# Turning P for two heads with one DMA transpose, a shorter drain, and full-height operands for two small matmuls

## The chip, the cores and the metric

The kernel runs on one core of one Trainium2 chip. The metric is the device time of one execution in microseconds (us). A core has TensorE (PE, matmuls; PEld is its weight load), VectorE (DVE), ScalarE (ACT), GpSimd (POOL), and SyncE (SP), which here issues every DMA. SBUF is the core's on-chip memory; matmul results land in PSUM, in eight banks.

## The reference

Three layers run one after the other on x (4 batches of 128 rows, width 512), each added to x:

```python
x = x + cross_attention(layernorm(x), ctx)   # ctx: 4 x 2048 x 512, 16 heads of 64, q and k RMS-normed,
                                             # keys past a batch's length masked
x = x + self_attention(layernorm(x))         # qkv with a bias, causal over 128 rows, output projection with a bias
x = x + ffn(layernorm(x))                    # 512 -> 1536 -> 512, gated, 4-bit weights and 16-bit activations by rounding
```

In the cross attention, K and V of each batch are `ctx @ Wk` and `ctx @ Wv`, the scores are `q k^T / 8`, P is their softmax over 2048 keys, the head's output is `P @ V`, and the heads' outputs are multiplied by Wo. Nearly all of the arithmetic is there: 4 x 2048 rows of context go through two 512 x 1024 projections.

## The kernel before

Every fp32 operand of a matmul is split into a high and a low fp16 part, and each product is three matmuls: high by high, high by low, low by high. Each stage (`cross_attention`, `self_attention`, `feed_forward`) is a block: one hand-written instruction list for each engine, tied by semaphores, and a barrier of all engines at its end.

**The loop over slots.** Cross attention goes over 4 batches, 8 groups of two heads and 4 chunks of 512 keys. That is 128 projections (`PROJS`), each spread over two slots, so there are 256 slots with projections; a part n is one head of one chunk, and there are 256 parts (`PARTS`). Eight parts (two heads, four chunks) are a unit. In slot s each engine does the steps whose lag fits: PE projects half a chunk of K and V (24 matmuls of 256 columns, L144 to L146), multiplies P by V for part s - 18 (`values`, `PV_LAG`, L824 to L826), and in odd slots makes the scores of a chunk for both heads (L868). In between, DVE masks the scores and takes their maximum (L703), ACT takes the exponential (L597) and copies it to fp16, the high half (L620), and POOL subtracts for the low half (L513). SP turns P with a DMA transpose of the 1024 columns (high and low) of one part (L397), into one of three buffers, and PE reads it as the stationary operand of `values`. Once in a unit, `values` opens with a matmul of zeros into its PSUM bank (L820), whose operands have one row each. K takes a way of its own: DVE sums its squares (L718), POOL takes the root (L523), DVE scales K (L724), and another DMA transpose (L404) turns it. ACT's high half of a part waits until the DMA transpose of the part three before has landed.

**What shares the queue.** SP's list also holds, in program order, the loads of the context, of the queries of a unit (`q_now`, L434) and of weights, and the storing of prepared weights in DRAM. Where an instruction waits, all behind it wait.

**The drain.** Projections end with slot 255, P by V of the last part comes in slot 273. The last 16 parts are turned by PE instead (L888), copied out of PSUM by DVE (L785). Two 512-column matmuls in each of five slots (L876) have no other use than to keep PE working. From slot 262 on (`OUT_FIRST`) PE also does the output projection of the first three batches, a quarter of a batch (six matmuls of 512 columns, L905 to L907) in each slot. The tiles of Wo for it come back from DRAM after slot 255, because they go where the context's low half lies. The block ends when the last unit's output has been divided (L684, L687), split (L643, L548) and sent through a DMA transpose (L459).

**Self attention** starts with the query and key projections (L1094 to L1096), has the last batch's output projection after seven of them (L1119), and adds the value bias with two matmuls of one-row operands ahead of each of the eight value projections (L1106, L1107). The attention of each batch goes through DMA transposes of P (L990) and of the output (L995), and its output projection (L1119) reads the latter.

## Time and profile before

| | |
|---|---|
| median of 3 runs | 1226.51 us (1225.75 to 1233.3) |
| the profiled execution's own time | 1228.04 us |
| its span, first to last instruction | 1226.1 us |
| PE busy | 1161.4 us, 95% of the span |
| DVE, ACT, POOL busy | 814.8, 735.0, 874.3 us |
| cross attention's loop, drain | to about 926 us, to about 971 us |
| self attention, feed-forward | to about 1093 us, to the end |

A matmul is pipelined: the next one starts before the last one's result is complete. So the cost of a matmul in a dense stretch is read from the distance between two starts, and not from its duration. Idle time of an engine matters only where another engine then waits for it.

### The profile page before, as it was taken

To read this page: it belongs to the slowest core of one execution; us is meant where nothing else is said; L and a number is where in the kernel's file an instruction comes from. 1 tells how busy PE (TensorE), PEld (TensorE's weight loads), DVE (VectorE), ACT (ScalarE), POOL (GpSimd) and SP (SyncE) were. 2 spreads that over 40 slices of the span, in tenths; PEclk is the share of its full clock that TensorE was granted. 3 is DMA by queue.
4 is the path that set the end of the run, shared out by engine and by line. 5 is a ranking of instruction groups with operands and counts; after the bars stand their busy time and mean duration, and the time that the engine had idled before them with its cause. 6 is when DMAs were issued, how large, how long until landed. Compare 5 with 4: busy or idle time off the path is not lost. (4 is left out here: it accounts for less than half of the span.)

```text
span 1226.1 us, 31362 instructions
## 1 busy us (share of the span) xinstructions
PE 1161.4 (95%) x11841; PEld 876.1 (71%) x11845; DVE 814.8 (66%) x1780; ACT 735.0 (60%) x1329; POOL 874.3 (71%) x750
## 2 busy tenths in 40 slices
PE   6899999999999999999999999999998899979958
PEld 4677777877888888788888878788885667534423
DVE  5778777697766678676666877666655444542772
ACT  5366655775767667666666776667666336512760
POOL 2689999888888898788888888898887423510510
PEclk9999999999999999999999999999999999989979
DMA  6579999999999999999999998999999533972000
GB/s 208 147 136 187 210 179 192 187 227 207 185 208 193 199 189 217 236 178 202 199 189 203 215 206 178 198 182 216 191 161 238 152 88 70 236 163 39 1 1 35
DMA packets 562345, 209.98 MB, mean 171 GB/s; under 512 B 506770, under 2 KB 529298, under 8 KB 562196
## 3 DMA queue, kind: packets, MB, share of 16 engines
q1 hardware_dynamic: 562196, 207.98, 84.4%
q8 instruction: 95, 1.56, 0.5%
q14 instruction: 54, 0.44, 0.1%
HBM read 66.27 MB, written 23.07 MB: 73 GB/s over the span
## 5 line engine op out<-in xcount | busy, mean ns | idle before, releaser
L144 PE MATMUL pair<-arena 128*128 128x256 f16 x2048 | 559.8, 273 | 15.6 <-DVE arena L655 7.8
L146 PE MATMUL pair<-arena 128*128 128x256 f16 x2048 | 558.9, 273 | 0.0
L145 PE MATMUL pair<-arena 128*128 128x256 f16 x2048 | 558.8, 273 | 0.0
L513 POOL TENSOR_TENSOR p_parts<-probs,p_parts 128x512 f16<-128x512 f32 x256 | 307.7, 1208 | 19.8 <-ACT p_parts L620 19.4
L523 POOL TENSOR_TENSOR k_rinv<-k_ms,half_neg 128x8 f32<-128x8 f32 x128 | 226.3, 1768 | 103.4 <-DVE k_ms L718 102.6
L144 PEld LDWEIGHTS pair<-arena 128*128 128x128 f16 x2048 | 200.2, 98 | 90.7 <-issue 47.7
L703 DVE CUSTOM_DVE_ANT_0 probs<-bank,mask 128x512 f32<-128x512 f32 x256 | 175.1, 684 | 114.8 <-PE bank L868 110.1
L620 ACT ACTIVATE p_parts<-probs 128x512 f16<-128x512 f32 x256 | 160.9, 629 | 100.7 <-DMA pt<-p_parts 89.2
L146 PEld LDWEIGHTS pair<-arena 128*128 128x128 f16 x2048 | 200.4, 98 | 23.7
L145 PEld LDWEIGHTS pair<-arena 128*128 128x128 f16 x2048 | 200.4, 98 | 20.8
L597 ACT ACTIVATE probs<-probs,neg_max 128x512 f32<-128x512 f32 x256 | 182.9, 714 | 8.7 <-DVE neg_max L712 8.7
L624 ACT ACTIVATE k_lh<-k_n 128x512 f16<-128x512 f32 x128 | 80.3, 627 | 152.0 <-DVE k_n L724 151.5
L518 POOL TENSOR_TENSOR k_lh<-k_n,k_lh 128x512 f16<-128x512 f32 x128 | 162.3, 1268 | 10.7 <-ACT k_lh L624 10.6
L724 DVE TENSOR_TENSOR k_n<-pair,k_rinv 128x512 f32<-128x512 f32 x128 | 88.3, 690 | 72.1 <-issue 45.1
L824 PE MATMUL bank<-v_hi,pt 128*128 128x65 f16 x1024 | 119.7, 193 | 2.8 <-DMA pt<-p_parts 2.8
L825 PE MATMUL bank<-v_lo,pt 128*128 128x65 f16 x1024 | 119.6, 194 | 0.0
L826 PE MATMUL bank<-v_hi,pt 128*128 128x65 f16 x1024 | 118.5, 193 | 0.0
L868 PE MATMUL bank<-kt,q_now 64*128 64x512 f16 x744 | 101.9, 379 | 7.2 <-DVE chunk_max L703 4.5
L824 PEld LDWEIGHTS bank<-v_hi,pt 128*128 128x128 f16 x1024 | 94.8, 97 | 10.5 <-DMA pt<-p_parts 4.7
L825 PEld LDWEIGHTS bank<-v_lo,pt 128*128 128x128 f16 x1024 | 94.8, 97 | 2.9
L826 PEld LDWEIGHTS bank<-v_hi,pt 128*128 128x128 f16 x1024 | 95.2, 98 | 0.0
L588 ACT ACTIVATE k_sq<-pair 128x512 f32<-128x512 f32 x128 | 75.1, 586 | 31.9 <-PE pair L146 31.1
(276 smaller groups left out, 1878.0 us busy)
## 6 DMA issues: line engine op xcount, KB each, us to landing
raws<-in_ctx_t_dram SPq DMA_DIRECT2D x64, 256.0 KB, 3.3
side_kept<-side_parts SPq DMA_DIRECT2D x40, 256.0 KB, 3.7
arena<-side_kept SPq DMA_DIRECT2D x40, 256.0 KB, 4.5
w_kept<-ffn_turned SPq DMA_DIRECT2D x36, 256.0 KB, 3.4
side_raw<-in_w_qkv_dram SPq DMA_DIRECT2D x24, 256.0 KB, 3.3
arena<-w_kept SPq DMA_DIRECT2D x24, 256.0 KB, 4.0
pt<-p_parts SPq DMA_TRANSPOSE x240, 3.7
ffn_raw<-in_w_gate_dram SPq DMA_DIRECT2D x12, 256.0 KB, 3.6
```

Of the source, the lines that this page charges most:

```text
L144: nc.tensor.matmul(to, x_hi[k], w_hi[k], start=(k == 0), stop=False)
L145: nc.tensor.matmul(to, x_hi[k], w_lo[k], start=False, stop=False)
L146: mm = nc.tensor.matmul(to, x_lo[k], w_hi[k], start=False, stop=(k == n - 1))
L513: nc.gpsimd.tensor_tensor(p_parts[n % PTS][:, 1, :], probs[n % PROBS][:, :], p_parts[n % PTS][:, 0, :], ALU.subtract).then_inc(p_lo_done, 1)
L518: nc.gpsimd.tensor_tensor(k_lh[(d - 1) % 2][:, 1, :], k_n[:, :, :, :].rearrange("p t h e -> p (t h e)"), k_lh[(d - 1) % 2][:, 0, :], ALU.s ...
L523: nc.gpsimd.tensor_tensor(k_rinv[d % 2][:, :], k_ms[d % 2][:, :], half_neg[:, 0:2 * TILES], ALU.pow).then_inc(k_rinv_done, 1)
L597: nc.scalar.activation(probs[n % PROBS][:, :], probs[n % PROBS][:, :], ACT.Exp, scale=S_SCALE, bias=neg_max[head_of(n) % 4][:, 0:1]).then_ ...
L620: nc.scalar.activation(p_parts[n % PTS][:, 0, :], probs[n % PROBS][:, :], ACT.Copy).then_inc(p_hi_done, 1)
L703: nc.vector.tensor_tensor_reduce(probs[m % PROBS][:, :], scores[h][:, :], mask[:, k, :], 1.0, LOWEST, ALU.add, ALU.max, chunk_max[h][:, k: ...
L824: nc.tensor.matmul(to, hi, v_hi[at % VS][:, t, h, :], start=False, stop=False)
L825: nc.tensor.matmul(to, hi, v_lo[at % VS][:, t, h, :], start=False, stop=False)
L826: mm = nc.tensor.matmul(to, lo, v_hi[at % VS][:, t, h, :], start=False, stop=(n % 8 == 7 and t == TILES - 1))
```

## The change

- P of both heads of a chunk is turned by one DMA transpose of 2048 columns, issued once both low halves are there. `values` comes one slot later (`PV_LAG` 19), P has four buffers in two pairs instead of three, and V ten instead of eleven.
- The tiles of Wo are laid out so that each one replaces two tiles of the context, and are loaded one in a slot from slot 249 on. The output projections start at slots 258, 262 and 266, and slot 257 alone keeps its two idle matmuls.
- The last unit's division, split and transpose move to the start of self attention's block.
- The operands of the zero matmul have 128 rows, not one. The high and the low part of the value bias stand in two rows of one 128-row operand (the rest is multiplied by zero), so one matmul adds both.

```diff
-SCORE_LAG, EXP_LAG, PV_LAG = 7, 15, 18
-CTX_RAWS, KTS, VS, PROBS, PTS, QS = 4, 3, 11, 10, 3, 3
+SCORE_LAG, EXP_LAG, PV_LAG = 7, 15, 19
+CTX_RAWS, KTS, VS, PROBS, PTS, QS = 4, 3, 10, 10, 4, 3
...
-OUT_FIRST, NORM_AT = (262, 266, 270), (266, 270)
+OUT_FIRST, NORM_AT, WO_FIRST = (258, 262, 266), (262, 266), 249
...
-        wo_at = arena[:, 24576:32768].rearrange("p (a k n) -> p a k n", a=2, k=GROUPS)
+        wo_at = arena[:, 24576:32768].rearrange("p (k a n) -> p a k n", a=2, k=GROUPS)
...
-        p_parts = [sb(f"p_parts{i}", [P, 2, CHUNK], F16, c) for i in range(PTS)]
-        pt = [sb(f"pt{i}", [P, 2 * TILES, P], F16, c) for i in range(PTS)]
+        pair_parts = [sb(f"pair_parts{i}", [P, 2, 2, CHUNK], F16, c) for i in range(PTS // 2)]
+        pair_turned = [sb(f"pair_turned{i}", [P, 2, 2 * TILES, P], F16, c) for i in range(PTS // 2)]
+        p_parts = [pair_parts[i // 2][:, i % 2, :, :] for i in range(PTS)]
+        pt = [pair_turned[i // 2][:, i % 2, :, :] for i in range(PTS)]
...
-        zeros = sb("zeros", [1, 2 * VW], F16, c)
+        zeros = sb("zeros", [P, 2 * VW], F16, c)
...
-        LAST = PARTS + PV_LAG + 4
+        LAST = PARTS + PV_LAG
 
         def whole_unit(lag, slot):
 
             n = part(PV_LAG + lag, slot)
-            return n // 8 if n is not None and n % 8 == 7 else None
+            return n // 8 if n is not None and n % 8 == 7 and n < PARTS - 1 else None
...
-                if (n := part(EXP_LAG + 1, slot)) is not None and n < PE_TURNS:
+                if (n := part(EXP_LAG + 1, slot)) is not None and n < PE_TURNS and n % 2 == 1:
+                    at = n // 2 % 2
                     sp.wait_ge(p_lo_done, n + 1)
                     wait(sp, pv_done, n - PTS + 1)
-                    sp.dma_start_transpose(pt[n % PTS][:, :, :],
-                                           p_parts[n % PTS][:, :, :].rearrange("p a k -> p (a k)")).then_inc(pt_in[n % PTS], 16)
+                    sp.dma_start_transpose(pair_turned[at][:, :, :, :].rearrange("p h a q -> p (h a) q"),
+                                           pair_parts[at][:, :, :, :].rearrange("p h a k -> p (h a k)")).then_inc(pt_in[at], 16)
...
+                if 0 <= (j := slot - WO_FIRST) < GROUPS:
+                    if j == 0:
+                        for i in range(2):
+                            sp.wait_ge(side_kept_done[i], 16 * SIDES // 2)
+                    sp.wait_ge(proj_done, PARTS - GROUPS + 1 + j)
+                    sp.dma_start(side_home(j), side_kept[j].rearrange("p (a n) -> p a n", a=2)).then_inc(side_in[j // 4], 16)
                 if slot == PARTS:
                     sp.wait_ge(proj_done, PARTS)
-                    for i in range(2):
-                        sp.wait_ge(side_kept_done[i], 16 * SIDES // 2)
-                for j in range(2 * (slot - PARTS), 2 * (slot - PARTS) + 2):
-                    if 0 <= j < DRAINED:
+                for j in range(GROUPS + 2 * (slot - PARTS), GROUPS + 2 * (slot - PARTS) + 2):
+                    if GROUPS <= j < DRAINED:
...
-                        wait(act, pt_in[n % PTS], 16 * (n // PTS))
+                        wait(act, pt_in[n // 2 % 2], 16 * (n // PTS))
...
-                        pe.wait_ge(pt_in[n % PTS], 16 * (n // PTS + 1))
+                        pe.wait_ge(pt_in[n // 2 % 2], 16 * (n // PTS + 1))
...
-                        nc.tensor.matmul(bank[7][:, 0:2 * VW], zeros[0:1, 0:P], zeros[0:1, :], start=True, stop=False)
+                        nc.tensor.matmul(bank[7][:, 0:2 * VW], zeros[:, 0:P], zeros[:, :], start=True, stop=False)
...
-                        pe.wait_ge(k_n_done, PROJS)
-                        pe.wait_ge(v_lo_done, PROJS)
+                        pe.wait_ge(k_n_done, PROJS - (b < 2))
+                        pe.wait_ge(v_lo_done, PROJS - (b < 2))
...
-        ones = sb("ones", [P, P], F16, c)
-        bv_row = [t[0:1, :, :].rearrange("p h e -> p (h e)") for t in o_n]
-        bv_hi, bv_lo = (sb(n, [P, E], F16, c) for n in ("bv_hi", "bv_lo"))
+        two_rows = sb("two_rows", [P, P], F16, c)
+        bv_row = [t[:, :, :].rearrange("p h e -> p (h e)") for t in o_n]
+        bv_parts = sb("bv_parts", [P, E], F16, c)
...
-                sp.dma_start(bv_row[i], g["b_qkv"][2 * E + D * i:2 * E + D * (i + 1)].partition_broadcast(1)).then_inc(bv_in, 16)
+                sp.dma_start(bv_row[i], g["b_qkv"][2 * E + D * i:2 * E + D * (i + 1)].partition_broadcast(P)).then_inc(bv_in, 16)
...
+            sp.wait_ge(last_lo_done, 1)
+            sp.dma_start_transpose(ot[:, B - 1, :, GROUPS - 1, :], last_parts[:, :, :].rearrange("p a n -> p (a n)")).then_inc(ot_in[1], 16)
...
+            nc.gpsimd.memset(two_rows[:, :], 0.0).then_inc(zeroed, 1)
             nc.gpsimd.memset(v_hi[:, :, :, HD:VW], 1.0).then_inc(ready, 1)
             nc.gpsimd.memset(v_lo[:, :, :, HD:VW], 0.0).then_inc(ready, 1)
-            pool.wait_ge(zeroed, 2)
+            pool.wait_ge(zeroed, 3)
+            for i in range(2):
+                pool.wait_ge(zeroed, 3 + i)
+                nc.gpsimd.affine_select(out=two_rows[:, :], in_=two_rows[:, :], compare_op=ALU.not_equal, fill=1.0, base=-32 * i,
+                                        pattern=[[0, P]], channel_multiplier=1).then_inc(zeroed, 1)
...
+            pool.wait_ge(last_hi_done, 1)
+            nc.gpsimd.tensor_tensor(last_parts[:, 1, :], last_o[:, :, :].rearrange("p h e -> p (h e)"), last_parts[:, 0, :],
+                                    ALU.subtract).then_inc(last_lo_done, 1)
...
+                if at[key] == 1:
+                    pe.wait_ge(last_o_done, 1)
...
-                nc.tensor.matmul(to[:, :], ones[0:1, :], bv_hi[0:1, n * D:(n + 1) * D], start=True, stop=False)
-                nc.tensor.matmul(to[:, :], ones[0:1, :], bv_lo[0:1, n * D:(n + 1) * D], start=False, stop=False)
+                nc.tensor.matmul(to[:, :], two_rows[:, :], bv_parts[:, n * D:(n + 1) * D], start=True, stop=False)
...
-            act.wait_ge(ready, 5)
+            act.wait_ge(last_o_done, 1)
+            act.wait_ge(ot_in[1], 16 * (B * GROUPS // 2 - 1))
+            nc.scalar.activation(last_parts[:, 0, :], last_o[:, :, :].rearrange("p h e -> p (h e)"), ACT.Copy).then_inc(last_hi_done, 1)
...
+            nc.vector.reciprocal(last_rec[:, :], last_new[:, :, HD]).then_inc(last_rec_done, 1)
+            dve.wait_ge(last_rec_done, 1)
+            nc.vector.tensor_tensor(last_o[:, :, :], last_new[:, :, 0:HD], last_rec[:, :].unsqueeze(2).to_broadcast([P, 2, HD]),
+                                    ALU.mult).then_inc(last_o_done, 1)
```

SP's list around the end of a unit, before (pt and kt are the turned P and K, `q_now` the next unit's queries, `ot` a unit's turned output):

```order
L404 DMA_TRANSPOSE kt<-k_lh 128x8x128
L397 DMA_TRANSPOSE pt<-p_parts 128x8x128
L434 DMA q_now<-q_kept 128x2x128
L452 DMA side_raw<-in_wo_dram 128x512
L455 DMA side_kept<-side_parts 128x1024
L459 DMA_TRANSPOSE ot<-o_parts 128x2x128
L397 DMA_TRANSPOSE pt<-p_parts 128x8x128
L404 DMA_TRANSPOSE kt<-k_lh 128x8x128
```

and now:

```order
L408 DMA_TRANSPOSE kt<-k_lh 128x8x128
L446 DMA_TRANSPOSE ffn_turned<-row_parts 128x8x128
L401 DMA_TRANSPOSE pair_turned<-pair_parts 128x16x128
L438 DMA q_now<-q_kept 128x2x128
L456 DMA side_raw<-in_wo_dram 128x512
L459 DMA side_kept<-side_parts 128x1024
L408 DMA_TRANSPOSE kt<-k_lh 128x8x128
```

Two transposes of P to one of K have become one; the queries' load stands right behind it, as it stood behind that of the odd part.

DVE's list in the drain, around the last two maxima (L703, now L711) and the first batch's sum (L793, now L801), before:

```order
L703 ISA probs,chunk_max<-bank,mask 128x512
L703 ISA chunk_max 128x1
L708 TENSOR_REDUCE head_max<-chunk_max 128x1
L712 TENSOR_SCALAR neg_max<-head_max 128x1
L785 COPY pt<-bank 128x1024
L785 COPY pt<-pair 128x1024
```

and now:

```order
L793 COPY pair_turned<-pair 128x1024
L801 SCALAR_TENSOR_TENSOR resid<-pair,resid 128x512
L804 BN_STATS ln_stats<-resid 128x6
L806 BN_AGGR ln_mean_var<-ln_stats 128x2
L711 ISA probs,chunk_max<-bank,mask 128x512
L711 ISA chunk_max 128x1
L716 TENSOR_REDUCE head_max<-chunk_max 128x1
```

The first batch's sum now stands ahead of the last maximum, and no longer four copies behind it.

SP's list where cross attention ends (the branches are the end of one block and the start of the next), before:

```order
L472 DMA arena<-side_kept 128x2x512 x2
L464 DMA_TRANSPOSE raws<-row_parts 128x8x128
L459 DMA_TRANSPOSE ot<-o_parts 128x2x128
L153 UNCONDITIONAL_BRANCH
L976 UNCONDITIONAL_BRANCH
L979 DMA att_o_n<-in_b_qkv_dram 1x512 x2
L980 DMA b_out_rows<-in_b_out_dram 128x512
```

and now:

```order
L463 DMA_TRANSPOSE ot<-o_parts 128x2x128
L468 DMA_TRANSPOSE raws<-row_parts 128x8x128
L155 UNCONDITIONAL_BRANCH
L987 UNCONDITIONAL_BRANCH
L990 DMA att_o_n<-in_b_qkv_dram 128x512 x2
L991 DMA b_out_rows<-in_b_out_dram 128x512
L1014 DMA_TRANSPOSE ot<-o_parts 128x2x128
```

The last unit's transpose has moved from ahead of the block's end to behind the next block's first three loads.

## Rows read from the trace of the kernel before

**Rows 1.** Windows: us, busy time (count) of each engine, granted clock, DMA share, GB/s.
```profile
100.00:920.00 820.00, 808.86 (x9067) 659.97 (x9065) 589.97 (x1316) 553.41 (x982) 716.51 (x573) 1.00 1.02 198
1046.00:1076.00 30.00, 27.75 (x272) 14.73 (x270) 18.12 (x36) 14.95 (x37) 14.28 (x16) 1.00 1.07 237
```
**Rows 2.** Waits of PE from 100 to 920 us: total us, times, longest.
```profile
PE bank L824 <- DMA pt<-p_parts: 2.8, 6, 0.7
PE bank L868 <- DMA q_now<-q_kept: 1.6, 2, 1.1
```
**Rows 3.** Timeline of PE around a zero matmul: start, duration, instruction.
```profile
602.99 0.27 PE L145 MATMUL pair<-arena 128*128 128x256 f16 x1
603.10 0.27 PE L146 MATMUL pair<-arena 128*128 128x256 f16 x1
603.30 0.23 PE L820 MATMUL bank<-zeros 1*128 1x130 f16 x1
603.46 0.20 PE L824 MATMUL bank<-v_hi,pt 128*128 128x65 f16 x1
```
**Rows 4.** SP's transposes of P, 1024 columns (L397): issue in ns, who waited, landing.
```profile
L397 SPq DMA_TRANSPOSE pt<-p_parts x240: 1231/1272/3078, 69.5 to 926.1; - x120
  ACT p_parts L620: 89.2, 68
DMA to landing us min/median/max: 3.0/3.7/6.1
```
**Rows 5.** The same view for the transposes of a unit's output, 256 columns (L459).
```profile
DMA to landing us min/median/max: 2.3/3.7/5.9
```
**Rows 6.** Timeline: the low half of odd part 151 (POOL), and its P by V (PE).
```profile
618.10 1.15 POOL L513 TENSOR_TENSOR p_parts<-probs,p_parts 128x512 f16<-128x512 f32 x1
...
626.82 0.27 PE L146 MATMUL pair<-arena 128*128 128x256 f16 x1
626.93 0.19 PE L824 MATMUL bank<-v_hi,pt 128*128 128x65 f16 x1
```
**Rows 7.** Timeline of PE in the drain, the last three scores, with the wait ahead.
```profile
929.43 0.82 PE L868 MATMUL bank<-kt,q_now 64*128 64x512 f16 x6 [1.63 <-DVE chunk_max L703]
...
934.74 0.82 PE L868 MATMUL bank<-kt,q_now 64*128 64x512 f16 x6 [1.14 <-DVE chunk_max L703]
...
939.27 0.80 PE L868 MATMUL bank<-kt,q_now 64*128 64x512 f16 x5 [1.12 <-DVE chunk_max L703]
```
**Rows 8.** Timeline where cross attention ends and self attention starts.
```profile
966.29 0.38 PE L907 MATMUL pair<-arena,ot 128*128 128x512 f16 x1
...
967.79 1.24 SPq L459 DMA_TRANSPOSE ot<-o_parts  x1
...
971.00 0.37 PE L1094 MATMUL bank<-raws,arena 128*128 128x256 f16 x1 [4.33 <-PEq L90]
```
**Rows 9.** Timeline where self attention ends and the feed-forward layer starts.
```profile
1091.40 0.69 DVE L1333 TENSOR_REDUCE x_tops<-raws 128x1 f32<-128x512 f32 x1
...
1093.04 0.55 SPq L1468 DMA_DIRECT2D wd<-w_kept  x1
```
**Rows 10.** Windows of three stretches, columns as in rows 1.
```profile
925.80:929.20 3.40, 2.00 (x34) 1.25 (x32) 1.82 (x4) 2.92 (x5) 1.95 (x3) 1.00 1.02 186
...
970.20:973.60 3.40, 2.60 (x13) 1.84 (x14) 1.57 (x3) 0.00 (x0) 2.71 (x9) 0.50 0.20 63
...
1076.00:1079.40 3.40, 3.40 (x10) 1.20 (x9) 0.03 (x1) 0.02 (x1) 1.15 (x1) 0.50 0.89 43
```
**Rows 11.** Timeline of PE ahead of the third output projection of self attention.
```profile
1075.51 0.38 PE L1119 MATMUL bank<-arena,ot 128*128 128x512 f16 x1 [2.15 <-issue]
```
**Rows 12.** Timeline of PE around the first value bias.
```profile
998.29 0.27 PE L1096 MATMUL bank<-raws,arena 128*128 128x256 f16 x1
998.49 0.38 PE L1106 MATMUL bank<-bv_hi,ones 1*128 1x512 f16 x1
...
999.02 0.39 PE L1110 MATMUL bank<-arena,raws 128*128 128x512 f16 x1
```

More of the change, by code:

```diff
@@ L129, in program @@
             o_parts = [sb(f"o_parts{i}", [P, 2, P], F16, attn) for i in range(2)]
+            o_rec = [sb(f"o_rec{i}", [P, 2], F32, attn) for i in range(2)]
+            o_n = [sb(f"o_n{i}", [P, 2, HD], F32, attn) for i in range(2)]
             row_parts = [sb(f"row_parts{i}", [P, 2, D], F16, attn) for i in range(2)]
@@ L157, in cross_attention @@
             g[n] for n in ("resid", "ot", "xt", "wo_at", "w_qkv_at", "side_kept", "side_in", "ot_in", "xt_in", "o_parts", "bqk"))
-        o_rec = [sb(f"o_rec{i}", [P, 2], F32, c) for i in range(2)]
-        o_n = [sb(f"o_n{i}", [P, 2, HD], F32, c) for i in range(2)]
+        o_rec, o_n = g["o_rec"], g["o_n"]
         side_raw = [sb(f"side_raw{i}", [P, D], F32, c) for i in range(2)]
@@ L239, in cross_attention @@
         kt_in = sems(c, "kt_in0 kt_in1")
-        pt_in = sems(c, " ".join(f"pt_in{i}" for i in range(PTS)))
+        pt_in = sems(c, "pt_in0 pt_in1")
         v_hi_done, v_lo_done = sems(c, "v_hi_done v_lo_done")
@@ L679, in _ @@
                 d = slot // 2 - 1
-                if (n := part(PV_LAG + 1, slot)) is not None and n % 8 == 7:
+                if (n := part(PV_LAG + 1, slot)) is not None and n % 8 == 7 and n < PARTS - 1:
                     u = n // 8
@@ L919, in self_attention @@
         HALF, TURNED = 2 * P, 11
+        last_o, last_rec, last_parts = g["o_n"][1], g["o_rec"][1], g["o_parts"][1]
+        last_new = bank[7][:, 0:2 * VW].rearrange("p (h v) -> p h v", h=2)
         NORMS = [("out", 2), ("out", 3)] + [("again", b) for b in range(B)]
@@ L956, in self_attention @@
         w_out_in = sems(c, "w_out_in0 w_out_in1")
+        last_rec_done, last_o_done, last_hi_done, last_lo_done = sems(c, "last_rec_done last_o_done last_hi_done last_lo_done")
         pt_in = sems(c, " ".join(f"att_pt_in{i}" for i in range(3)))
@@ L1024, in _ @@
             nc.gpsimd.memset(beyond[:, :, :], 0.0).then_inc(zeroed, 1)
-            nc.gpsimd.memset(ones[:, :], 1.0).then_inc(ready, 1)
+            nc.gpsimd.memset(two_rows[:, :], 0.0).then_inc(zeroed, 1)
             nc.gpsimd.memset(v_hi[:, :, :, HD:VW], 1.0).then_inc(ready, 1)
             nc.gpsimd.memset(v_lo[:, :, :, HD:VW], 0.0).then_inc(ready, 1)
-            pool.wait_ge(zeroed, 2)
+            pool.wait_ge(zeroed, 3)
[3 more added lines that the diff above has]
+                                        pattern=[[0, P]], channel_multiplier=1).then_inc(zeroed, 1)
             nc.gpsimd.affine_select(out=less[:, :], in_=less[:, :], compare_op=ALU.not_equal, fill=-2.0 ** 20, base=0,
@@ L1102, in values @@
                 if b == 0 and n == 0:
-                    pe.wait_ge(ready, 5)
+                    pe.wait_ge(zeroed, 5)
+                    pe.wait_ge(ready, 4)
                     pe.wait_ge(bv_lo_done, 2)
                 to, s, cols = placed(("v", b, n)), slice(b * P, (b + 1) * P), slice(2 * E + n * D, 2 * E + (n + 1) * D)
-                nc.tensor.matmul(to[:, :], ones[0:1, :], bv_hi[0:1, n * D:(n + 1) * D], start=True, stop=False)
-                nc.tensor.matmul(to[:, :], ones[0:1, :], bv_lo[0:1, n * D:(n + 1) * D], start=False, stop=False)
+                nc.tensor.matmul(to[:, :], two_rows[:, :], bv_parts[:, n * D:(n + 1) * D], start=True, stop=False)
                 for k in range(KD):
@@ L1262, in _ @@
                     for h in range(2):
-                        nc.scalar.activation(bv_hi[0:1, D * h:D * (h + 1)], bv_row[h], ACT.Copy, scale=W2_UP).then_inc(bv_hi_done, 1)
+                        nc.scalar.activation(bv_parts[:, D * h:D * (h + 1)], bv_row[h], ACT.Copy, scale=W2_UP).then_inc(bv_hi_done, 1)
                 if i == 10:
                     x_high(1)
+            act.wait_ge(ready, 4)
             high_v(0, 0)
@@ L1369, in _ @@
                         dve.wait_ge(bv_hi_done, h + 1)
-                        nc.vector.scalar_tensor_tensor(bv_lo[0:1, D * h:D * (h + 1)], bv_row[h], W2_UP, bv_hi[0:1, D * h:D * (h + 1)], ALU.mult,
-                                                       ALU.subtract).then_inc(bv_lo_done, 1)
+                        nc.vector.scalar_tensor_tensor(bv_parts[32:64, D * h:D * (h + 1)], bv_row[h][32:64], W2_UP,
+                                                       bv_parts[32:64, D * h:D * (h + 1)], ALU.mult, ALU.subtract).then_inc(bv_lo_done, 1)
                 if i == 8:
```

## The prediction

> **What bounds the kernel now.** I read the windows first. From 100 to 920 us PE is busy for 808.9 of 820 us and the clock stays at its full level [rows 1], so there a change is worth what it takes from PE's own list; POOL, next, is busy for 716.5. The waits of PE say how little is left for a faster supply: in those 820 us it waits 2.8 us for turned P and 1.6 us for the queries [rows 2]. Then I looked for what a busy share hides, by the distance between two starts in the timeline [rows 3]. The places where PE really stands lie after the loop: three waits for the maxima in the drain, 4.33 us at the end of cross attention, and a wait of 2.15 us in self attention, each with its rows below.
>
> **The zero matmul.** A projection matmul starts 0.11 us after the one before; the one-row zero matmul starts 0.20 us after its predecessor, and the next starts 0.16 us behind it [rows 3]. With 128 rows it should take its share of columns, 130/256 of 0.11, which is 0.06, and the start ahead of it should go back to 0.11. That saves 0.09 + 0.10 = 0.19 us. There is one in each of 32 units, 30 of them in the dense loop: **-5.8 us** (between nothing and -6.2). I take the full saving because the same 0.09 us stands ahead of the one-row bias matmul too, and matmuls of equal height follow one another without it [rows 3]; the bias is taken up below.
>
> The Trainium skill ("TensorE: Matmul & The Clock Gate", Part 2, step-by-step) speaks against this: time goes by the columns, and "row count K doesn't matter here". By that rule this term would be nothing, and the sum about 6 us longer. The trace differs where the height changes from one matmul to the next, 0.20 against 0.11 us, and I go by the trace.
>
> **One transpose for two parts.** SP issues 120 instead of 240; each issue takes 1.23 us or more [rows 4]. That frees 1.2 us of SP in every two slots (one slot is about 3.4 us), but SP does no work of the loop's bound. The bytes are the same. The landing of 1024 columns takes 3.0 us at least, of 256 columns 2.3 [rows 4, 5]; another 1024 columns add between 0.7 x 1024/768 = 0.9 us and, if all behind the issue doubles, 3.0 - 1.2 = 1.8. So 2048 columns land after 3.9 to 4.8 us at best; with the 0.7 us that the median lies above the least, 4.6 to 5.5. I take 5. The even part's P by V is one slot later than before, and so stands where the odd part's stood: in the example its start is 626.93 - 619.25 = 7.7 us behind the end of the odd part's low half [rows 6]. 5 us and a wait of up to 2 for SP's turn fit into this; the odd part has a slot more. ACT's wait for the part three before, 89.2 us over 68 waits [rows 4], goes for odd parts and gets up to 1.5 us longer for even ones; behind it POOL works off a backlog, which covers that. The queries' load stands right behind the pair and gets up to 1.5 us more of data ahead of it; PE waits for it twice, by at most 1.1 us [rows 2], and the saved 1.2 us of issue is on the other side. Fewer waits for P (2.8 us) against somewhat longer ones for the queries: **-1 us**, between -4 and +6 (about six units at 1 us each). Ten V buffers cost nothing: ACT's copy of chunk d needs the projection of slot 2d + 1 in any case, and PE has read chunk d - 10 in slot 2d, ahead of it in its list.
>
> **The drain.** Only differences count. Eight of ten idle matmuls go, each 0.22 us, twice the 0.11 of 256 columns: -1.8. The output projection of the first batch, 24 x 0.22 = 5.3 us, now stands where PE waited 1.14 and 1.12 us for the maxima [rows 7]: -2.3; the wait of 1.63 us comes ahead of slot 258 and stays. The second zero matmul of the drain gives -0.2. Against that, the eighth tile of Wo can be asked for only when the last projection is done, and lands about when PE is ready for it: +0.5. The last five slots have no projection beside them, and the last copies of P from PSUM are in the open: +0.5. The part moved out of the loop into the drain is neutral. The first batch's sum, now ahead of the last maximum on DVE, delays the exponentials of one head by some 2 us; they are two slots early. So PE ends 3.3 us sooner relative to the loop.
>
> Then the block's end. Before, PE stood for 4.33 us, because the issue of the last unit's transpose ran until 967.79 + 1.24 = 969.03, and PE restarted at 971.00 [rows 8]: 2.0 us from the last instruction to the next block. At the next block's end it is 0.95 us (1092.09 to 1093.04) [rows 9]. Now PE's own P by V is the last work, so its gap is 1.0 to 2.0 us; with 1.4, **-2.9**. The drain together: **-6.2 us**, between -2.5 and -8.5. What is late next is PE itself.
>
> **The clock.** After the 4.33 us gap the granted clock is at its lower level until 973.6 [rows 10], and twelve matmuls start 0.21 instead of 0.11 us apart. After the gap of 1.63 us it stayed full, after that of 2.15 us it fell [rows 7, 10, 11]. A gap of 1.4 us is on the good side: **-1.2**, and nothing if it falls all the same.
>
> **Self attention.** The value bias takes 999.02 - 998.49 = 0.53 us and 0.09 ahead of it [rows 12]; one matmul of 128 rows takes 0.22. That is 0.40 for each of eight. The first three come before attention proper is under way: **-1.2**. The other five lie ahead of the wait of 2.15 us for a turned output [rows 11], in a stretch where the DMA engines are full, 1.07 [rows 1], and only lengthen it; all eight would be -3.2. The moved work of the last unit is DVE 0.5, ACT 0.3, POOL 0.4 us and a transpose of at least 2.3 us [rows 5]; behind POOL's preparations it lands about 7.5 us into the block, and its reader comes after seven projections of 12 x 0.11, at 9.2 us. It costs nothing unless these are late by 1.7 us.
>
> **The sum**: -5.8 - 1.0 - 6.2 - 1.2 - 1.2 = -15.4 on the profiled execution's 1228.0 us (span 1226.1), so 1212.6. That execution lay 1.5 us above the median of 1226.5, so I predict **1211 us**.
>
> **The rivals.** (a) The longer transpose takes back what the zero matmul gives: queries and P late by 0.5 to 1 us in a good part of the units, +6 to +8 on my sum, 1217 to 1219. For it speaks the DMA share of 1.02 [rows 1], against it the room of 7.7 us. Chance 0.17. (b) Height makes no difference, the rule above read as a mechanism of this kernel: the 0.20 and 0.16 us belong to the change of target bank and not to the one row. Then the zero matmuls give nothing (+6.0 with the drain's) and the bias matmuls 0.22 each instead of 0.40 (+0.5): 1217.5. Against it, P by V goes to another bank too and follows at 626.93 - 626.82 = 0.11 where no zeros stand between [rows 6]. Chance 0.07. (c) Slower than before: one transpose of 2048 columns has a price of its own, so that it lands more than the 7.7 us after the odd low half. From there every pair makes PE wait, and 120 waits cost 12 us for each 0.1 us. The point is a landing of about 7 us from issue, twice the median of 3.7 or nearly so; at a mean wait of 0.25 us it is 1211 + 30 = 1241. Against it, 256 columns and 1024 differ by 0.7 us [rows 4, 5]. Chance 0.06. (d) The freed SP queue lets the stalls in the loop go altogether, PE has 11 us of non-busy time there [rows 1], and more of the bias is passed on: -4 to -7, 1204 to 1207. Chance 0.15. (e) My sum within 3 us, 0.55.
>
> The range holds (e), (d) and most of (a) and (b): **1204 to 1220**. What can be told from no change here is about 1%, 12.3 us: faster means below 1214.2. That is (e) for the most part, and (d): **0.65**. The same: (a), (b), the upper end of (e), **0.29**. Slower: (c), **0.06**.
>
> **What would show it.** In the profile after: zero matmuls 0.11 us behind their predecessor and 0.06 ahead of the next; landings of the 2048-column transposes near 5 us and PE's waits for them below 5 us in total; ACT's waits for P fewer than 68; PE standing 1 to 2 us at the end of cross attention, at the full clock afterwards; self attention's start 6 us sooner relative to the loop's end; a wait ahead of the third output projection of self attention longer than 2.15 us. Wrong would be the sum if PE waits for P in every second slot, if the first output projection waits for Wo by more than 2 us, or if self attention ends no sooner relative to its start than before.

## The result, and the profile after

| | before | after |
|---|---|---|
| median | 1229.45 us (20 runs, 1225.75 to 1235.31) | 1225.86 us (20 runs, 1222.39 to 1230.9) |
| ratio | | 0.997, 95% interval 0.9957 to 0.9983 |
| span of the profiled execution | 1226.1 us | 1222.2 us |

(The 20 runs of before take in the three shown ahead, whose median was 1226.51.) The change is worth 3.6 us, not 15. The forecast of 1211 us, with 1204 to 1220 around it, was wrong. Four stages of the two profiled executions show where; a stage ends with the start of the next PE instruction named. (Loop: to the last projection matmul. Drain: to the first matmul of self attention. Self attention: to the last one before the feed-forward layer.)

| us | loop | drain | self attention | feed-forward |
|---|---|---|---|---|
| before | 925.9 | 45.1 | 120.9 | 134.2 |
| after | 923.5 | 45.6 | 116.5 | 136.6 |
| predicted difference | -6.8 | -6.2 | -2.4 | 0 |
| difference | -2.4 | +0.6 | -4.4 | +2.4 |

**The zero matmul** does what the sum says. PE's timeline of the kernel after, start, duration and instruction:

```profile
524.67 0.27 PE L148 MATMUL pair<-arena 128*128 128x256 f16 x1
524.78 0.22 PE L828 MATMUL bank<-zeros 128*128 128x130 f16 x1
524.84 0.19 PE L832 MATMUL bank<-v_hi,pair_turned 128*128 128x65 f16 x1
```

It starts 0.11 us behind the projection and the next follows 0.06 later, where it was 0.20 and 0.16 in [rows 3]. Waits of PE from 100 to 920 us, the same view as [rows 2] (total us, times, longest):

```profile
PE bank L876 <- issue: 5.2, 4, 1.9
PE bank L832 <- DMA pair_turned<-pair_parts: 4.4, 7, 1.0
PE bank L828 <- DMA pair_turned<-pair_parts: 3.6, 4, 1.5
PE bank L876 <- DMA q_now<-q_kept: 0.7, 1, 0.7
PE pair L146 <- issue: 0.3, 1, 0.3
```

The other rows of that view for the kernel before, beside the two of [rows 2]:

```profile
PE pair L144 <- issue: 2.9, 10, 0.4
PE pair L144 <- DVE k_n L724: 1.5, 2, 0.8
PE bank L868 <- issue: 1.0, 1, 1.0
PE bank L868 <- DVE chunk_max L703: 0.6, 2, 0.3
PE bank L820 <- DMA pt<-p_parts: 0.3, 1, 0.3
```

PE waits 8.0 us for turned P, where it was 3.1 (2.8 and 0.3). The waits ahead of the scores (L876, before L868) that the profile puts down to "issue" have grown from 1.0 to 5.2, and they are waits for the queries: each of the four ends 0.1 us after a load of `q_now` has landed in the trace, as does the one that the profile puts down to that load. So the queries cost 5.9 us, where it was 2.6. Together these waits are 8.2 us longer. The rest, mostly ahead of the projections, went from 5.0 to 0.3 us. So of the 5.9 us that 30 zero matmuls give, the loop lost 3.5 net and kept 2.4. The transposes of a pair, the view of [rows 4]:

```profile
L401 SPq DMA_TRANSPOSE pair_turned<-pair_parts x120: 1317/2170/5239, 76.6 to 925.4; - x120
  ACT pair_parts L628: 139.4, 87
DMA to landing us min/median/max: 4.2/4.7/7.4
```

The landing of 4.7 us at the median is what I took (5). What I did not count on is the issue, which holds SP for 2.17 us at the median and 5.24 at the most. One of the places where PE pays, SP, POOL and PE around 711 to 718 us:

```profile
708.67 1.15 POOL L521 TENSOR_TENSOR pair_parts<-probs,pair_parts 128x512 f16<-128x512 f32 x1
...
710.97 4.73 SPq L401 DMA_TRANSPOSE pair_turned<-pair_parts  x1
...
718.31 0.23 PE L828 MATMUL bank<-zeros 128*128 128x130 f16 x1 [1.48 <-DMA pair_turned<-pair_parts]
```

The odd part's low half is done at 709.82 and PE wants the even part at 716.83, 7.0 us later. SP's turn comes after 1.15 us, and issue with landing takes 7.3 from there: 8.5 us in all, so PE stands for 1.48.

**The drain.** PE and SP of the kernel after, behind the last projection (923.49):

```profile
926.98 0.82 PE L876 MATMUL bank<-kt,q_now 64*128 64x512 f16 x6 [1.63 <-DVE chunk_max L711]
...
929.80 0.20 PE L832 MATMUL bank<-v_hi,pair_turned 128*128 128x65 f16 x1 [1.01 <-DMA pair_turned<-pair_parts]
...
934.22 0.59 PE L913 MATMUL pair<-arena,ot 128*128 128x512 f16 x1 [3.08 <-DMA arena<-side_kept]
...
957.92 0.22 PE L828 MATMUL bank<-zeros 128*128 128x130 f16 x1 [0.71 <-DVE o_n L695]
...
969.14 0.27 PE L1116 MATMUL bank<-raws,arena 128*128 128x256 f16 x1 [1.60 <-PEq L90]
```
```profile
924.70 0.57 SPq L475 DMA_DIRECT2D arena<-side_kept  x1
925.37 2.95 SPq L401 DMA_TRANSPOSE pair_turned<-pair_parts  x1
928.36 0.58 SPq L475 DMA_DIRECT2D arena<-side_kept  x1
929.03 1.24 SPq L408 DMA_TRANSPOSE kt<-k_lh  x1
930.32 0.57 SPq L475 DMA_DIRECT2D arena<-side_kept  x1
```

The first output projection (L913) stands 3.08 us for the eighth tile of Wo. SP asks for it only at 930.32, 6.8 us after the last projection has started: two other tiles, a transpose of K (1.24 us) and the last pair's transpose, which holds SP for 2.95 us, stand ahead of it on SP's list. The last pair costs another 1.01. The gap at the block's end is 1.60 us, where 1.4 was forecast (4.33 in [rows 8]). Windows, with the granted clock as the third number from the end, of the whole loop, of the stretch behind the stand, of the start of self attention, of the stretch that ran at half clock in [rows 10], and of the start of the feed-forward layer:

```profile
100.00:920.00 820.00, 805.66 (x9098) 663.19 (x9097) 579.81 (x1323) 553.10 (x986) 712.44 (x575) 1.00 1.02 200
932.70:939.50 6.80, 5.28 (x27) 2.27 (x28) 0.16 (x1) 2.95 (x7) 3.84 (x5) 0.50 1.03 287
966.00:972.00 6.00, 4.34 (x67) 3.82 (x65) 3.11 (x7) 0.83 (x3) 2.90 (x10) 1.00 0.47 115
1069.00:1080.00 11.00, 9.31 (x47) 4.43 (x46) 5.30 (x11) 0.63 (x1) 2.73 (x5) 1.00 0.72 186
1086.30:1096.50 10.20, 6.85 (x18) 2.68 (x18) 4.17 (x14) 2.44 (x4) 0.20 (x1) 0.50 1.02 180
```

The stand is followed by 6.8 us at 1.2 GHz; output matmuls start 0.43 us apart there, not 0.22. The start of self attention is at full clock.

**Self attention** gained more than predicted. Ahead of its third output projection PE waits

```profile
1070.94 0.38 PE L1141 MATMUL bank<-arena,ot 128*128 128x512 f16 x1 [1.69 <-issue]
```

where it was 2.15 in [rows 11], and the clock did not fall behind it. In the feed-forward layer nothing was changed, but the clock was low for 10.2 us at its start, and for 6.8 before:

```profile
1093.10:1099.90 6.80, 4.02 (x11) 1.76 (x12) 4.17 (x14) 1.84 (x3) 0.15 (x1) 0.50 0.88 176
```

### The profile page after: what moved, and what is told of

Its sections match the earlier page's. It is cut to its first block and busy times, and to the rows that moved or that the text cites. A ratio compares the mean times of both kernels' runs of the same rounds, so it can differ in the third digit from the quotient of the medians.

```text
span 1222.2 us, 31088 instructions
## 1 busy us (share of the span) xinstructions
PE 1152.0 (94%) x11825; PEld 876.5 (72%) x11829; DVE 804.0 (66%) x1780; ACT 731.9 (60%) x1329; POOL 870.0 (71%) x750
## 5 line engine op out<-in xcount | busy, mean ns | idle before, releaser
L521 POOL TENSOR_TENSOR pair_parts<-probs,pair_parts 128x512 f16<-128x512 f32 x256 | 307.0, 1203 | 33.6 <-ACT pair_parts L628 33.2
L711 DVE CUSTOM_DVE_ANT_0 probs<-bank,mask 128x512 f32<-128x512 f32 x256 | 175.3, 685 | 154.2 <-PE bank L876 145.5
L628 ACT ACTIVATE pair_parts<-probs 128x512 f16<-128x512 f32 x256 | 160.9, 629 | 148.6 <-DMA pair_turned<-pair_parts 139.4
L526 POOL TENSOR_TENSOR k_lh<-k_n,k_lh 128x512 f16<-128x512 f32 x128 | 158.0, 1234 | 12.1 <-ACT k_lh L632 12.0
L832 PE MATMUL bank<-v_hi,pair_turned 128*128 128x65 f16 x1024 | 119.4, 193 | 5.4 <-DMA pair_turned<-pair_parts 5.4
L833 PE MATMUL bank<-v_lo,pair_turned 128*128 128x65 f16 x1024 | 119.6, 194 | 0.0
L834 PE MATMUL bank<-v_hi,pair_turned 128*128 128x65 f16 x1024 | 118.5, 193 | 0.0
L876 PE MATMUL bank<-kt,q_now 64*128 64x512 f16 x744 | 102.5, 381 | 7.5 <-issue 5.2
L832 PEld LDWEIGHTS bank<-v_hi,pair_turned 128*128 128x128 f16 x1024 | 95.5, 97 | 11.6 <-DMA pair_turned<-pair_parts 7.7
L833 PEld LDWEIGHTS bank<-v_lo,pair_turned 128*128 128x128 f16 x1024 | 94.8, 97 | 2.7
L834 PEld LDWEIGHTS bank<-v_hi,pair_turned 128*128 128x128 f16 x1024 | 95.2, 98 | 0.0
```

Source lines behind the costliest of these rows:

```text
L521: nc.gpsimd.tensor_tensor(p_parts[n % PTS][:, 1, :], probs[n % PROBS][:, :], p_parts[n % PTS][:, 0, :], ALU.subtract).then_inc(p_lo_done, 1)
L526: nc.gpsimd.tensor_tensor(k_lh[(d - 1) % 2][:, 1, :], k_n[:, :, :, :].rearrange("p t h e -> p (t h e)"), k_lh[(d - 1) % 2][:, 0, :], ALU.s ...
L628: nc.scalar.activation(p_parts[n % PTS][:, 0, :], probs[n % PROBS][:, :], ACT.Copy).then_inc(p_hi_done, 1)
L711: nc.vector.tensor_tensor_reduce(probs[m % PROBS][:, :], scores[h][:, :], mask[:, k, :], 1.0, LOWEST, ALU.add, ALU.max, chunk_max[h][:, k: ...
L832: nc.tensor.matmul(to, hi, v_hi[at % VS][:, t, h, :], start=False, stop=False)
L833: nc.tensor.matmul(to, hi, v_lo[at % VS][:, t, h, :], start=False, stop=False)
```

## The experiments

Two theories. **Loop**: the pair's transposes supply P too late in crowded places, and that takes back most of what the zeros give. **Drain**: the stand for Wo and the low clock behind it take back most of what the shorter drain gives. Against both: the 0.20 us of the zero matmul can't be had, since another engine or the DMA queue paces the loop. Ratios are to the kernel before, timed on the same chip in between (medians 1229.8 to 1231.7 us); 0.1% is 1.2 us. The stage times are those of one profiled execution each:

| us | ratio (95%) | median | loop | drain | self attention | feed-forward |
|---|---|---|---|---|---|---|
| before_again | | 1231.45 (one run) | 929.0 | 45.1 | 120.8 | 134.5 |
| zeros_alone | 0.9974 (0.9951 to 0.9998) | 1227.03 | 927.0 | 44.9 | 123.3 | 134.2 |
| pair_alone | 1.0047 (1.0027 to 1.0068) | 1236.56 | 932.2 | 48.2 | 120.9 | 134.3 |
| single_turns | 0.9944 (0.9921 to 0.9967) | 1223.59 | 922.2 | 41.7 | 117.5 | 134.8 |
| pair_of_two | 0.9989 (0.9969 to 1.0008) | 1229.0 | 930.7 | 45.6 | 116.4 | 134.3 |
| wo_half | 0.995 (0.9929 to 0.9972) | 1224.42 | 925.8 | 42.4 | 117.0 | 136.2 |
| single_wo_half | 0.9933 (0.9906 to 0.996) | 1224.45 | 929.7 | 40.8 | 117.4 | 134.7 |
| single_lag18 | 0.9899 (0.9875 to 0.9923) | 1218.84 | 922.0 | 41.5 | 118.6 | 134.7 |
| four_buffers | 0.9908 (0.9886 to 0.993) | 1219.64 | 922.4 | 40.0 | 119.9 | 136.5 |
| zeros_one_row | 0.9933 (0.9909 to 0.9956) | 1222.93 | 926.7 | 40.9 | 120.8 | 135.2 |
| qkv_later | 0.9875 (0.9848 to 0.9902) | 1215.16 | 924.1 | 38.9 | 119.0 | 134.7 |
| pair_later | 0.994 (0.9927 to 0.9953) | 1223.41 | 925.7 | 40.6 | 117.0 | 134.3 |

**zeros_alone.** The kernel before with

```diff
-        zeros = sb("zeros", [1, 2 * VW], F16, c)
+        zeros = sb("zeros", [P, 2 * VW], F16, c)
...
-                        nc.tensor.matmul(bank[7][:, 0:2 * VW], zeros[0:1, 0:P], zeros[0:1, :], start=True, stop=False)
+                        nc.tensor.matmul(bank[7][:, 0:2 * VW], zeros[:, 0:P], zeros[:, :], start=True, stop=False)
```

> The kernel before with the zero matmul's operands 128 rows high, nothing else. Theory 'loop': the 0.20 us that each of about 30 zero matmuls in the loop gives are real, and what the changed kernel lost again comes from its other parts; so this edit alone gives 5 to 6 us, 1223.5 to 1224.5 against 1229.5. Rival 'absorbed': POOL, ACT or the DMA queue paces the loop as soon as PE is 0.2 us faster in a unit, and the stalls come back whatever the transposes look like; then at most 2 us, 1227.5 or above.

0.26% faster, 3.2 us, with an interval that takes in both theories. Its profiled execution, 1231.38 us, was its slowest. It is settled further below (zeros_one_row).

**pair_alone.** The kernel before with lag 19, four P and ten V buffers, and the pair's transpose, as in the change's diff.

> The kernel before with the pair transposes, P by V one slot later, four P and ten V buffers, nothing else. Theory 'loop': the transpose of 2048 columns holds SP for 2.2 us and lands later, PE waits for P and for queries more often: 4 us slower in the loop, about 1 us more in the drain, 1233 to 1235. Rival 'absorbed': the pair costs nothing by itself, 1229 to 1231 (the drain's slot at most).

0.47% slower, 5.8 us (3.3 to 8.4): more than expected, and against the rival. The waits of PE for P, from 100 to 920 us, and the transposes:

```profile
PE bank L827 <- DMA pair_turned<-pair_parts: 4.8, 7, 1.4
PE bank L871 <- issue: 4.7, 5, 2.1
PE bank L823 <- DMA pair_turned<-pair_parts: 3.9, 2, 2.2
```
```profile
L400 SPq DMA_TRANSPOSE pair_turned<-pair_parts x120: 1317/2522/4859, 76.2 to 931.9; - x120
DMA to landing us min/median/max: 4.2/4.8/7.5
```

So the losses come with the pair and its lag, with the one-row zeros in place; the waits put down to "issue" end with the landing of queries here too. Behind two of its waits in the loop the clock was low for 3.4 us each. The drain, with the old output projections, is 3.1 us longer: it has the slot that the lag adds, and a wait for a maximum of 1.84 us (1.14 in [rows 7]), behind which the clock fell as well:

```profile
942.30:945.50 3.20, 3.20 (x30) 2.33 (x29) 1.30 (x3) 1.69 (x3) 2.62 (x3) 0.50 1.23 215
```

**single_turns.** The changed kernel with one transpose for each part again; lag 19 and the buffers stay:

```diff
-                if (n := part(EXP_LAG + 1, slot)) is not None and n < PE_TURNS and n % 2 == 1:
+                if (n := part(EXP_LAG + 1, slot)) is not None and n < PE_TURNS:
...
-                    sp.dma_start_transpose(pair_turned[at][:, :, :, :].rearrange("p h a q -> p (h a) q"),
-                                           pair_parts[at][:, :, :, :].rearrange("p h a k -> p (h a k)")).then_inc(pt_in[at], 16)
+                    sp.dma_start_transpose(pt[n % PTS][:, :, :],
+                                           p_parts[n % PTS][:, :, :].rearrange("p a k -> p (a k)")).then_inc(pt_in[n % PTS], 16)
```

> The changed kernel with one transpose of 1024 columns for each part again, everything else kept (P by V a slot later, four P and ten V buffers). Theory 'loop': PE's waits for P go from 8.0 us to 3 or less, values of slot 255 start 3 to 4 us sooner, 1222 against 1225.9. Rival 'absorbed': loop and total as in the changed kernel within 1 us.

About 3 us under the changed kernel (0.9944 against 0.997, with intervals that touch). Waits for P are gone from the loop, but it has new ones: two for the queries, 4.4 us in all, and two for maxima, 2.5. The loops of the two traces end only 1.3 us apart. The drain is 3.9 us shorter: without the long issue of the last pair, the eighth tile of Wo is late by 2.25 us and not 3.08, and the clock stays full behind it. So this run does not price the loop alone.

**wo_half.** The changed kernel, with the second four tiles of Wo waited for where they are read:

```diff
-                            pe.wait_ge(side_in[i], 64)
+                            pe.wait_ge(side_in[0], 64)
+                    if first == 4:
+                        pe.wait_ge(side_in[1], 64)
```

> The changed kernel, but the first output projection waits for tiles 4 to 7 of Wo only two slots later, where it reads them. Theory 'drain': the stand of 3.08 us goes, and with it the low clock of 6.8 us behind it: 3 + 3 us, 1220 against 1225.9. Rival 'moved': the waits for the maxima (1.14 and 1.12 us before) come back in its place and the clock falls all the same: 1 us or less, 1225.

The stand and the low clock are gone, and the drain is 3.3 us shorter; the whole is 2.5 us faster than the changed kernel by the ratios (0.995 against 0.997), which their intervals do not tell from nothing. It is less than half of what I expected, since a wait came in their place that neither theory had:

```profile
935.12 0.82 PE L876 MATMUL bank<-kt,q_now 64*128 64x512 f16 x6 [0.22 <-DVE chunk_max L711]
942.21 0.82 PE L876 MATMUL bank<-kt,q_now 64*128 64x512 f16 x6 [1.90 <-DMA kt<-k_lh]
```

**pair_of_two.** The changed kernel, with a pair turned by two transposes, one right behind the other:

```diff
-                    sp.dma_start_transpose(pair_turned[at][:, :, :, :].rearrange("p h a q -> p (h a) q"),
-                                           pair_parts[at][:, :, :, :].rearrange("p h a k -> p (h a k)")).then_inc(pt_in[at], 16)
+                    for h in range(2):
+                        sp.dma_start_transpose(pair_turned[at][:, h, :, :],
+                                               pair_parts[at][:, h, :, :].rearrange("p a k -> p (a k)")).then_inc(pt_in[at], 16)
```

> The changed kernel, but a pair is turned by two transposes of 1024 columns issued one behind the other once both low halves are there. Theory 'batch': what costs is that the even part waits for the odd one and that both move in one burst, not that one DMA does it; then as the changed kernel, 1225.9, with two issues of 1.25 us. Rival 'length': one transpose of 2048 columns is slow by itself (issue 2.17 us at the median, landing 4.7); then the even half lands earlier and it is near single_turns, 1223.

Not faster than the changed kernel (0.9989 against 0.997, with intervals that overlap), and clearly slower than single_turns (0.9944), so the rival "length" falls: two short issues bring nothing back while the even part waits for the odd one and both then move together. Which of these two costs, the wait or the burst, was not tested.

**before_again.** The kernel before, once more.

> The kernel before once more, for a second trace. The first one's loop ended at 926 us; two executions of the changed kernel's loop (after and wo_half, the same instructions up to slot 260) ended it at 923.5 and 925.8. If single traces differ by 2 to 3 us for the same work, this one ends its loop anywhere from 925 to 930, and terms below 2 us can't be read from one pair of traces.

Its loop ended 3.1 us later than in the first trace, with PE waiting 5.5 us for P instead of 3.1; drain and self attention agree within 0.1 us. So a pair of traces can't price a loop term under 3 us, and the first trace of the kernel before, on which the prediction stands, was the quicker of the two in the loop.

**single_wo_half, single_lag18.** The edits of single_turns and wo_half together; and the same with the loop of the kernel before:

```diff
-SCORE_LAG, EXP_LAG, PV_LAG = 7, 15, 19
-CTX_RAWS, KTS, VS, PROBS, PTS, QS = 4, 3, 10, 10, 4, 3
+SCORE_LAG, EXP_LAG, PV_LAG = 7, 15, 18
+CTX_RAWS, KTS, VS, PROBS, PTS, QS = 4, 3, 11, 10, 3, 3
```

> The changed kernel with both edits of before: one transpose for each part, and tiles 4 to 7 of Wo waited for two slots later. If the pair and the stand for Wo are separate losses, their gains add: single turns gave 6.3 us against the kernel before (medians), the stand for Wo was 2.25 us there, so about 8.5 us under the kernel before, 1221. Rival 'one bound': both edits free the same waiting, and this is no faster than single turns alone, 1223.5.

> As single_wo_half, but with the loop of the kernel before: P by V at lag 18, three P buffers, eleven V buffers. So it is the changed kernel with the pair undone altogether. Theory: the lag and the fourth buffer are worth little once turns are single (PE waited 2.8 us for turned P in the kernel before), but ACT waits again for the part three before: 1 to 2 us slower than single_wo_half in the loop, 2 us shorter in the drain, equal within 1.5 us. Rival: the fourth buffer was the part of the change that helped the loop; then it is 3 us slower or more.

The first is no better than single_turns by the medians, the second is 0.34% faster still, at the edge of what their intervals can tell; I did not expect it. In the profiled execution of the first PE waits 8.0 us for the queries in the loop (2.5 in the second), and the clock falls behind such waits, for 17 us in all (never in the loop of the second); medians and profiles point the same way. The second differs from wo_half by the pair with its lag and buffers alone: 0.9899 against 0.995, so these cost 0.5%, 6.3 us, as in pair_alone.

**four_buffers.** single_lag18 with four P buffers and ten V buffers:

```diff
-CTX_RAWS, KTS, VS, PROBS, PTS, QS = 4, 3, 11, 10, 3, 3
+CTX_RAWS, KTS, VS, PROBS, PTS, QS = 4, 3, 10, 10, 4, 3
```

> single_lag18 with four P and ten V buffers, lag 18 kept. single_wo_half, with lag 19 on top of this, was 0.3% slower than single_lag18, and PE waited 8 us for queries there, against 2.5. Theory 'buffers': with the fourth buffer ACT no longer waits for turned P (2.4 against 88.8 us), the transposes come earlier and the queries' load, behind them in SP's list, later: waits for queries of 5 us or more, 1222. Rival 'lag': values one slot later does it, and this is as single_lag18, 1219.

As single_lag18, with 0.5 us of waits for queries: the theory "buffers" falls. And ACT's waits for turned P, 86.3 us from 100 to 920 us in single_lag18, are 0.9 us here, without a gain: they cost nothing.

**zeros_one_row.** single_lag18 with the edit of zeros_alone taken back.

> single_lag18 with the zero matmul's operands one row high again. Alone in the kernel before, the edit gave 0.26%, between 0.02 and 0.49, so the 6.0 us of the prediction were neither shown nor excluded. Theory: full value, 6 us slower than single_lag18, 1225. Rival: half of it is taken up by waits for P and queries that are shorter when PE is slower, 3 us slower, 1222.

0.9933 against 0.9899: 4.1 us slower. From the second zero matmul to the last projection the traces give 811.4 us with one row, and 804.6, 805.9 and 804.7 us with 128 rows (single_lag18, qkv_later, four_buffers). In zeros_alone it was 810.6, its slowest run, against 813.0 and 813.5 in the two traces of the kernel before. So from there on the traces show about the full 5.9 us (5.5 to 6.8). Counted from the start of the execution they show less: the last projection comes at 926.7 us with one row, and at 922.0, 924.1 and 922.4 with 128, 2.6 to 4.7 us sooner, since these three came to their second zero matmul 2 to 3 us later. The runs show 3 to 4 us, and their intervals exclude neither all of the 5.9 nor next to nothing. How much of the saving is taken up by other waits stays open.

**qkv_later.** In single_lag18 the last K is late in the drain. PE, and SP's list ahead of it:

```profile
938.45 0.82 PE L873 MATMUL bank<-kt,q_now 64*128 64x512 f16 x6 [2.44 <-DMA kt<-k_lh]
```
```profile
927.55 0.56 SPq L472 DMA_DIRECT2D arena<-side_kept  x1
928.16 1.20 SPq L477 DMA_DIRECT2D arena<-side_kept  x2
929.41 0.61 SPq L447 DMA_DIRECT2D w_kept<-ffn_turned  x1
930.07 1.21 SPq L477 DMA_DIRECT2D arena<-side_kept  x2
931.37 1.82 SPq L405 DMA_TRANSPOSE kt<-k_lh  x1
```

```diff
-                for j in range(GROUPS + 2 * (slot - PARTS), GROUPS + 2 * (slot - PARTS) + 2):
+                for j in range(GROUPS + 3 * (slot - PARTS - 3), GROUPS + 3 * (slot - PARTS - 3) + 3):
```

> single_lag18, but the tiles of the query, key and value weights are loaded from slot 259 on, three in a slot, not from slot 256, two in a slot. In single_lag18 the last transpose of K stands on SP's list behind six such tiles, and PE waited 2.44 us for it at 938.45. Theory: those 2.4 us go, the drain (last projection to self attention) takes 39 us, as the prediction's sum wanted (45.1 less 6.2), and the time is 1216.5. Rival: the next wait (for a maximum, 1.1 us before) comes in its place, or self attention waits for its weights, then 1218 or more.

The wait is gone and nothing took its place. PE in the drain and at the start of self attention:

```profile
924.09 0.27 PE L148 MATMUL pair<-arena 128*128 128x256 f16 x1
...
927.58 0.82 PE L873 MATMUL bank<-kt,q_now 64*128 64x512 f16 x6 [1.63 <-DVE chunk_max L708]
...
929.78 0.20 PE L829 MATMUL bank<-v_hi,pt 128*128 128x65 f16 x1 [0.39 <-DMA pt<-p_parts]
...
963.01 0.27 PE L1115 MATMUL bank<-raws,arena 128*128 128x256 f16 x1 [1.59 <-PEq L90]
```

The drain takes 38.9 us, which is 45.1 less the 6.2 of the prediction. With 1215.16 us, 1.25% under the kernel before, this is the fastest version of all. (Beside single_lag18 it is 3 us, which the runs alone do not tell from nothing; the 2.6 us of the drain are read from the traces.)

**pair_later.** The changed kernel with the edits of wo_half and qkv_later.

> The changed kernel with its pair transposes, both repairs of the drain (wo_half and qkv_later), nothing else. Beside qkv_later it differs by the pair alone (lag 19, four P and ten V buffers). Theory: the pair costs what it did in the kernel before (pair_alone 0.47% slower) and beside single_lag18 (0.51%), 6 us: 1221.5. Rival: part of that price came from the drain's queue, where the pair's transposes stood beside the tiles of Wo; then 1218 or less.

0.994 against 0.9875: the pair and its lag cost 0.65%, 8 us (4 to 12), with the drain in order. The rival falls.

## Why the prediction was wrong, step by step

- **The zero matmul (-5.8).** The saving of 0.20 us each is exactly there in the starts of matmuls. Rival (b) falls. Its rule from the Trainium skill ("TensorE: Matmul & The Clock Gate", Part 2, step-by-step, of the weight load: "row count K doesn't matter here") does not hold in this trace where the height changes from one matmul to the next: 205 against 109 ns ahead of the zero matmul, and 158 against 57 behind it, at the medians of 32. By the runs the term is 3.2 to 4.1 us with wide bounds (0.2 to 6 in zeros_alone).
- **One transpose for two parts (-1): mis-sized, by 7 to 9 us.** Measured three times: +5.8 (pair_alone), +6.3 (single_lag18 beside wo_half), +8.0 (qkv_later beside pair_later). I had +6 as the upper end, and rival (a) described the mechanism, for P and for the queries, with a chance of 0.17. The first step that failed is "5 us and a wait of up to 2 for SP's turn fit into this": medians fitted into the room of one example, 7.7 us. But the issue of 2048 columns takes up to 5.2 us and more than 3 in 27 of 116 cases, the landing takes up to 7.4, and PE waited 11 times, 8.0 us where it was 3.1. I had the maxima of the 1024-column transposes in [rows 4] (3.08 and 6.1 us) and used only the median. The step on the queries failed too: "PE waits for it twice, by at most 1.1 us" was to be made good by the saved 1.2 us of issue, and became five waits of 5.9 us, up to 1.9 us each. The saved issues of SP bought nothing that PE waits for. ACT's waits for turned P, which were to become fewer than 68, became 87; four_buffers shows that such waits cost nothing by themselves. How the price divides between the joint transpose and the lag of 19 is not shown: with the lag kept, single transposes give back 2 to 3 us (single_turns, single_wo_half beside wo_half), the lag, without or with its buffers, is worth 3 to 4 (single_wo_half beside four_buffers and single_lag18), and none of these four differences is clear of noise by itself.
- **The drain (-6.2): a term of it and its condition were wrong.** "The eighth tile of Wo ... lands about when PE is ready for it: +0.5" failed: a stand of 3.08 us, with 6.8 us at half clock behind it. That clock cost about 2.5 us more, an estimate from wo_half, whose drain is 3.3 us shorter while its waits there are only 0.8 shorter (7.2 against 8.0). The last pair's transpose (1.01 us) and a wait for the division (0.71, where it was 0.4) are most of the rest of the 6.8 us by which the drain missed. I had named a wait for Wo of more than 2 us as a sign that the sum is wrong, and priced it at 0.5. When the stand was taken away, the next late load was the last K (1.90 to 2.44 us), behind five tiles and a stored piece of 256 KB each on SP's list. With both gone, the drain takes the predicted 38.9 us, but at lag 18 (qkv_later). With the pair and lag 19, as the prediction had it, it needs 40.6 (pair_later), with 1.3 us of wait for its last pair.
- **The clock (-1.2) and the value bias (-1.2).** Both came in the changed kernel: from the start of self attention to the wait ahead of the third value projection it is 2.0 us shorter, two bias pairs at 0.4 and 1.2 of clock. Another 1.7 us, by half of the 3.4 us that were at half clock in [rows 10], came because the clock did not fall behind the wait ahead of the third output projection. That was not argued, and it goes both ways: the 2.4 us longer start of the feed-forward layer has no cause in the change, and appears in four_buffers and wo_half too, and not in the others.
- **The sum.** The whole change without its pair, and with two small edits that put the drain's loads in order, gives 1.25%, 15.4 us (12 to 19): as much as I had forecast for the change as it stands. That the two agree to the tenth is luck: qkv_later has no pair (-1.0), its clock fell at the start of self attention (-1.2), and it has other terms that I did not forecast. In the traces of before and after the change gave 3.9 us and not 15.4. The drain missed by 6.8, the loop by 4.4, and the feed-forward layer took 2.4 more, while self attention gave 2.0 more. What was lost in drain and loop goes back to the one list of SP: P and queries that are late at its crowded places, and loads that stand on it in the wrong order.

## What to carry over

Check a new wait against the worst issue and landing in the trace and the tightest room, not against medians: a transfer with 5 us at the median and 7 us of room was late 11 times in 116. Where a load is moved close to its reader, write down the whole list of its queue between the two; the stall that is removed uncovers the next one on the same queue. And take two traces of the kernel before: its loop differed by 3 us between two executions, half of the largest term.

## What the runs showed of the hardware

- The issue of a DMA transpose on SP takes 1.23 us at the least for 1024 columns and 1.32 for 2048, but 1.27 and 2.17 at the median and 3.08 and 5.24 at the most ([rows 4], and the view of L401 in the kernel after). The landing is 3.0 us against 4.2 at the least, 1.2 us more for the second 1024 columns.
- After the gap of 1.6 us between cross attention and self attention the clock stayed at 2.4 GHz in the profiled executions of after, wo_half, pair_of_two, single_turns, single_wo_half and pair_later, and fell to 1.2 GHz in single_lag18, qkv_later, four_buffers and zeros_one_row, with gaps of 1.58 to 1.61 us. The latter have lag 18, and PE stood for another 0.42 us about 0.5 us ahead of the gap; the former have lag 19 and no such stand there. That this is the cause is not shown. The length of a stand alone does not tell either. In the drain the clock fell behind 1.84 us (pair_alone), 3.08 (after) and 3.2 (pair_of_two), and stayed full behind 2.25 (single_turns) and 2.44 (single_lag18). Two windows of qkv_later, the drain and the stretch behind the gap:

```profile
924.00:963.00 39.00, 34.68 (x460) 22.55 (x458) 24.54 (x52) 22.12 (x37) 26.18 (x29) 1.00 0.99 241
963.80:967.20 3.40, 3.40 (x19) 2.34 (x17) 1.51 (x4) 0.47 (x1) 2.84 (x9) 0.50 0.62 231
```

- Why values one slot later, with single transposes, make the queries late (8.0 us in single_wo_half, 0.5 in four_buffers) was not found; in single_wo_half the clock was low for 17 us of the loop, behind such waits.
